# Moving the second layer norm's row operations of the mixing stage from VectorE to ScalarE

## The reference

```python
x = L0_attn_a_x                                    # (4, 1024, 256) float32
x = x + attention(layernorm(x))                    # 16 heads of 16, has a residual of its own
x = x + ffn(layernorm(x))                          # ternary weights, 256 -> 256
x = x + memory(layernorm(x))                       # projections, causal convolutions, gates,
                                                   # a memory updated chunk by chunk
x = x + ffn(layernorm(x))

def layernorm(x, eps=1e-05):
    m, v = mean(x), var(x)                         # over the last axis
    return (x - m) / sqrt(v + eps)
```

## Time and profile before

| | |
|---|---|
| median of three runs | 1159.07 us |
| profiled execution | 1160.27 us |
| its span | 1157.8 us |
| mean granted clock of TensorE | 0.957 |
| TensorE busy | 1065.8 us (92%) |
| VectorE busy | 1000.0 us (86%) |
| ScalarE busy | 809.4 us (70%) |
| GpSimd busy | 244.0 us (21%) |

### The profile page before, as it was taken

One profiled execution on the slowest core, in us unless ns is written; L12 is line 12 of the kernel. 1 busy time (PEld: TensorE's weight loads), 2 busy tenths in 40 slices (PEclk: granted clock), 3 DMA queues, 4 the chain that ended last, 5 costly groups with the idle time before them and its releaser, 6 DMA issues. The chain is left out here.

```text
span 1157.8 us, 22154 instructions
## 1 busy us (share of the span) xinstructions
PE 1065.8 (92%) x8566; PEld 586.2 (51%) x8566; DVE 1000.0 (86%) x1467; ACT 809.4 (70%) x1655; POOL 244.0 (21%) x345
## 2 busy tenths in 40 slices
PE   5997799999999999999999999995799998999995
PEld 4885233333333333333333333334567765888984
DVE  7877999999999999999999999915499998569887
ACT  4462288888888888888888888880468686343443
POOL 6514300000000000000000000014234334565643
PEclk9997599999999999999999999997899997799998
DMA  7694404413431441343144230023134325634321
GB/s 270 159 338 162 55 13 75 67 33 54 67 57 31 75 67 33 54 67 60 27 75 67 41 54 12 20 91 95 37 111 141 116 79 166 191 84 133 102 74 54
DMA packets 87332, 101.55 MB, mean 88 GB/s; under 512 B 21884, under 2 KB 57212, under 8 KB 87228
## 3 DMA queue, kind: packets, MB, share of 16 engines
q1 hardware_dynamic: 86396, 98.56, 35.3%
q10 hardware_dynamic: 832, 1.58, 0.4%
HBM read 55.09 MB, written 43.88 MB: 85 GB/s over the span
## 5 line engine op out<-in xcount | busy, mean ns | idle before, releaser
L653 ACT ACTIVATE prob<-ps_s 128x512 f32<-128x512 f32 x1024 | 555.7, 597 | 115.1 <-PE ps_s L723 97.7
L674 DVE TENSOR_REDUCE maxes<-ps_m 128x2 f32<-128x1024 f32 x512 | 606.6, 1218 | 17.8 <-PE ps_m L712 14.6
L735 PE MATMUL ps_o<-prob,v_ones 128*32 128x256 f32 x4096 | 327.8, 392 | 7.8 <-issue 6.7
L723 PE MATMUL ps_s<-q_stack,k_stack 64*128 64x512 f32 x1024 | 261.0, 499 | 0.0
L712 PE MATMUL ps_m<-k_stack,q_stack 62*128 62x512 f32 x1024 | 219.2, 422 | 14.7 <-DVE maxes L674 11.0
L723 PEld LDWEIGHTS ps_s<-q_stack,k_stack 64*128 64x128 f32 x1024 | 99.7, 184 | 211.3 <-ACT prob L653 186.7
L735 PEld LDWEIGHTS ps_o<-prob,v_ones 128*32 128x32 f32 x4096 | 81.6, 108 | 191.6 <-issue 100.8
L615 POOL COPY v_ones<-v_all 128x512 f32<-128x512 f32 x16 | 9.8, 614 | 531.1 <-PE ps_o L735 531.1
L712 PEld LDWEIGHTS ps_m<-k_stack,q_stack 62*128 62x128 f32 x1024 | 101.0, 192 | 31.6 <-DVE maxes L674 23.5
L69 DVE BATCH_NORM_STATS2 p_stats<-x_all 128x6 f32<-128x256 f32 x124 | 43.5, 413 | 6.7 <-DMA x_all<-in_x_dram 5.9
L1138 DVE TENSOR_TENSOR x_all<-x_all,p_a 128x512 f32<-128x512 f32 x16 | 10.9, 681 | 42.9 <-POOL p_pre_q L971 30.5
(11 more groups left out here) (276 smaller groups left out, 1497.0 us busy)
## 6 DMA issues: line engine op xcount, KB each, us to landing
qk_parts<-p_parts SPq DMA_DIRECT2D x32, 512.0 KB, 7.1
q_stack<-qk_parts SPq DMA_DIRECT2D x96, 128.0 KB, 4.7
k_stack<-qk_parts SPq DMA_DIRECT2D x96, 128.0 KB, 7.8
oT<-o_sb SPq DMA_DIRECT2D x32, 256.0 KB, 3.9
x_all<-in_x_dram SPq DMA_DIRECT2D x8, 512.0 KB, 10.2
heads<-oT SPq DMA_DIRECT2D x16, 256.0 KB
inverse<-inverse_sums SPq DMA_DIRECT2D x16, 256.0 KB
out_dram<-x_all SPq DMA_DIRECT2D x7, 512.0 KB, 3.4
```

Of the source, the lines that this page charges most:

```text
L653: act.activation(prob[at % P_RING][:, h], ps_s[:, (GH * at + h) % S_RING], ACT.Exp, scale=HD ** -0.5).then_inc(exp_done, 1)
L674: dve.tensor_reduce(maxes[:, i // 2, i % 2], ps_m[:, i % M_PAIRS], AX.X, ALU.max).then_inc(m_taken, 1)
L723: pe.matmul(ps_s[:, (GH * (UNITS * slot + KT * qc + kt) + h) % S_RING], r32(k_st[slot][rows, pair, kt * P:(kt + 1) * P]), r32(q_st[slot][r ...
L735: ins = pe.matmul(ps_o[32 * h:32 * h + 32, queries], v_st[slot][:, kt, h], prob[(UNITS * slot + KT * qc + kt) % P_RING][:, h, queries], st ...
```

## The change

VectorE's `put_h` and its call are removed. ScalarE gets a `put_h` that computes the same as rstd * x + shift, with shift = -(mean * rstd), in four Identity activations with scale and bias taken from tiles. It is called between `means(it + 1)` and `keys_values(it)`. GpSimd makes the shift in two operations on 128 x 4 numbers, directly behind rstd. ScalarE's `put_h` waits for the shift and, from chunk 1 on, for the previous `turn_h`.

```diff
+    shift = sb("shift", [P, 2, TPC])
+    shift_ready, shift_steps = sem("shift_h"), sem("shift_steps")
...
+        def negative_means(n):
+            pool.wait_ge(rstd_h, n + 1)
+            pool.tensor_tensor(tmp[:, n % 2, 1], mv[:, n % 2, 1, :, 0], rstd[:, n % 2, 1], ALU.mult).then_inc(shift_steps, 1)
+            pool.wait_ge(shift_steps, n + 1)
+            pool.tensor_tensor(shift[:, n % 2], scalar(const, S_ZERO, [P, TPC]), tmp[:, n % 2, 1], ALU.subtract).then_inc(shift_ready, 1)
...
                 deviation(it + 2, 1, var_h, rstd_h)
+                negative_means(it + 2)
...
+        def put_h(n):
+            act.wait_ge(shift_ready, n + 1)
+            if n:
+                act.wait_ge(hT_turned, n)
+            for i in range(TPC):
+                ins = act.activation(hid[:, i], x_of(n)[:, i], ACT.Identity, bias=shift[:, n % 2, i:i + 1], scale=rstd[:, n % 2, 1, i:i + 1])
+            ins.then_inc(h_ready, 1)
...
                 means(it + 1)
+            if valid(it + 2):
+                put_h(it + 2)
...
-        def put_h(n):
-            dve.wait_ge(rstd_h, n + 1)
-            if n:
-                dve.wait_ge(hT_turned, n)
-            normalise(dve, x_of(n), mv[:, n % 2, 1], rstd[:, n % 2, 1], hid, h_ready)
...
                 lower_zT(it + 3)
-            if valid(it + 2):
-                put_h(it + 2)
```

## The result

The changed kernel takes 1193.2 us (median of four runs, 1192.09 to 1194.16) against 1159.2 before: 1.0289 times the time, 95% interval 1.0273 to 1.0305. It is slower by 34.0 us. I had forecast 22.4 us more, 1181.5, and a range up to 1191.0; the result lies 2 us above the range. The profiled execution took 1192.09 us, its span 1190.2, the mean granted clock 0.945.

The account below looks back on a forecast made before the run. The prediction took ScalarE's stretch, closed through TensorE with 0.1 us of slack, as the bound. Chunk losses of 20.45 us plus 2.0 for the clock gave +22.4, so 1181.5 us against the median of 1159.07; range 1172 to 1191.

Parts of the forecast that it names:

- What bounds the kernel: Mixing stage: ScalarE's run from second projection to first gates forms a closed loop with TensorE, 0.1 us of slack.
- Part 1: VectorE loses `put_h`, 1.37 us a round; gain taken as 0, bounds 0 and 0.6 us a round.
- Part 2: ScalarE gets `put_h` inside its closed stretch: four rows, 2.07 us, cost 1.9 us a round.
- Part 3: ScalarE waits for GpSimd's bias, its subtraction held by one scan; middle rounds pay 2.9 us including rows, bounds 1.9 and 4.0.
- The sum without the clock: Losses of `put_h` over chunks 0 to 7: 1.25 + 1.1 + 11.6 + 2.7 + 3.8 = 20.45 us.
- TensorE's clock: New gaps on TensorE may drop its clock to 1.2 GHz: +2.0 us, bounds 0 and 6.0.
- The granted clock falls in every round: Sign named in advance that the forecast would be wrong in size; no size of its own given.
- Bias never held: GpSimd's pair and VectorE's scan do not meet: 14 us more, 1173 without clock loss; chance 12%.
- both held: Both GpSimd operations for the bias stand behind scans: 27.3 us more, 1186 to 1192 with the clock; chance 14%.
- rows hidden in idle time: The four rows fall into ScalarE's idle time, some 5 us a round: 1159 to 1160.5; chance 4%.
- VectorE sets the pace: VectorE bounds the rounds, so the change is faster by up to 0.6 us in four rounds: 1156.7; chance 3%.
- table loads added: Identity on ScalarE needs eight more table loads of 1.28 us: 10.3 us more, 1191.8; chance 3%.

Follow-up runs that it names:

- e2: The kernel before, VectorE's `put_h` kept, with four unread Identity rows added on ScalarE between `means` and `keys_values`; 1179.6 us, ratio 1.0178.
- e5: The changed kernel reordered: ScalarE copies the gates ahead of `put_h`, TensorE puts `turn_h` between the halves of `out_products`; 1169.1 us, ratio 1.0079.
- e4: The kernel before, with VectorE's `put_h` cut to 32 of 256 columns per row; 1158.9 us, ratio 1.0001.
- e9: The changed kernel with TensorE's gaps filled by small transposes and the bias made by one VectorE operation; 1172.9 us, ratio 1.0121.
- e1: The changed kernel with small unread transposes filling TensorE's gaps before `turn_h`, `out_products` and the last two rounds' `projections`; 1180.7 us, ratio 1.0188.
- e11: The changed kernel with GpSimd's rstd and bias put ahead of `divide_heads` instead of behind it; 1188.1 us, ratio 1.0274.
- e6: The kernel before, with a one-column Sigmoid on ScalarE ahead of the wait for the first projection, moving the table load; 1158.7 us, ratio 0.9990.

## Why the prediction was wrong, step by step

- **What bounds the kernel: right.** ScalarE's stretch from the second projection to the first gates, closed through TensorE, with no slack. e2 shows it with nothing moved: rows that no one reads lengthen every round. e5 shows the other side: out of the stretch they cost at most 0.3 us a round.
- **Part 1, VectorE's relief worth 0: right** as far as e4 shows (1.0001), which takes away a third of `put_h`.
- **Part 2, rows on ScalarE: right.** 2.08 us for four, forecast 2.07. In sum 1.25 + 1.1 + 4 x 1.9 + 2 x 2.0 = 14.0 against 13.9 in e9. That the two agree to 0.1 us is partly luck: e9's stage is 15.9 us longer, and its middle rounds take 22.32 to 22.51 us, 2.1 to 2.2 more than before where I had 1.9.
- **Part 3, the wait for the bias: right in its mechanism, and nearly in size.** Product 0.20, subtraction 1.00, as told. My sum held 6.5 us for it (20.45 less 14.0); e1 less e9 gives 7.5, each against its own runs of before. ScalarE's waits in the middle rounds were smaller than the 0.9 I took where the scan of E started earlier (0.52 to 0.68), and larger in chunks 2 and 3 (1.20 and 1.62) by the link of e11, which I had left out although GpSimd's queue has `divide_heads` ahead of `deviation`. In chunk 7 the wait was 1.56, forecast 1.8.
- **The sum without the clock: right.** Forecast 20.45, e1 measured 21.4 (1180.7 less 1159.25), its middle rounds 22.9 to 23.3 us long, forecast 23.2.
- **TensorE's clock: this step failed.** I took 2.0 us of bounds 0 to 6.0; it was 12.5. Three things were wrong in it. The low stretches of the middle rounds last 6.8 and 3.4 us by turns, not always the 3.4 that I took from the one case of the earlier trace rows. They do not begin before `turn_h`, inside the wait for the gates, but at its end, in the gap behind it or 0.5 us into `out_products`, so that most of each falls on work that the loop waits for: 1.4 to 2.9 us a round in place of 0.65, and 2.6 and 2.9 in the last two rounds in place of at most 1.7 (7.97 and 8.34 us against 5.42). And chunk 1 pays too (5.30 us for `out_products` against 3.62). With 0.9 for `turn_h` of chunk 7 these parts make some 16.7 us, beside the 16.1 by which the stage is longer than in e1. My upper bound was built from the same one case, so the range inherited the error. "The granted clock falls in every round" was among my own signs of a wrong size, and it came.
- **What stays open: when the clock falls.** I ranked the gaps by their length, and the traces do not: it held over 2.21 us in e2 and fell with 2.03 and 2.13 in the rounds behind it.
- **The rivals.** Bias never held, both held, rows hidden in idle time, VectorE sets the pace, table loads added: none happened. ScalarE's timeline has no table load between `means` and `put_h`.

## What to carry to other kernels

An engine's idle share says nothing about what more work on it costs: follow its timeline from the point where it waits for another engine to the point where that engine waits for it, and if this stretch has no gap, everything put into it is paid in full; in this kernel the same work behind the copy that TensorE waits for, with TensorE's order changed to match, cost at most 0.3 us a round. When an edit opens gaps of 1 to 2 us on TensorE in every round, price a low clock in every one of them, not in a third, and on the work right behind the gap (here 1.4 to 2.9 us of a product of 3.69), and test it by filling the gap: here cheap extra matmuls took 12.5 us off. One low stretch in a trace gives neither its usual length nor the gap that brings it. When an operation is removed from one engine, look also at what moves forward into its place: here a scan moved under a small GpSimd operation and made it five times as long.

## What the runs showed of the hardware

- In a middle round of the changed kernel the granted clock fell to 1.2 GHz with gaps of 1.43 and 1.11 us and 1.09 us of matmuls between them. It stayed low for 6.8 us (916.1 to 923.0), although TensorE worked without a pause from 917.2 on; in the next round, with the same gaps to 0.01 us, it was low for 3.4 us.
- The length of a gap alone does not tell whether the clock falls. It fell with a gap of 2.13 us in e2 and held over one of 2.21 in the same execution. In the round of chunk 1, behind a gap of 1.25 to 1.26 us, it held in the kernel before and fell in e6 (at about 839.5, for 3.4 us). In e1, with gaps of 0.19 and 0.24 us, it stayed at 2.4 GHz.
- A GpSimd product or subtraction of 128 x 4 takes 0.20 us alone, 0.25 beside a VectorE operation with one tensor input, and beside a scan with two it stands until the scan's end (1.00). It works the other way too: a division on GpSimd that began first held such a scan for 0.94 us (2.16 instead of 1.22).
- DMA traffic at a share of 1.01 beside the 16 matmuls of `out_products` left their time at 3.69 us (e1).
